# Two Gram matrices mirrored through DRAM instead of by TensorE, the second one moved ahead of a projection tile, and the batch loop written out

## The reference, cut to what matters

```python
z_l = einsum('bnd,ed->bne', x, W_lang)
z_g = einsum('bnd,ed->bne', x, W_grav)
v   = einsum('bnd,ed->bne', x, W_V)
zn  = z_l / maximum(norm(z_l), EPS)
A_l = maximum(zn @ zn^T, 0) * not_eye
sq  = sum(z_g * z_g)
d2  = maximum(sq + sq^T - 2 * z_g @ z_g^T, 0)
A_g = exp(-d2 / (2 * sigma * sigma)) * not_eye
K   = w_l * rownorm(A_l * adj) + (1 - w_l) * rownorm(A_g * adj)
out = layernorm(x + (K @ v) @ W_O^T)
```

## Time and profile before

| | |
|---|---|
| runs | 1014.73 us median of 3 (1011.64 to 1014.81) |
| the profiled execution: its own time, its span | 1013.06 us, 1011.3 us |
| mean granted TensorE clock | 0.996 |
| busy: PE, PEld, DVE, ACT, POOL | 983.0, 845.0, 677.1, 327.0, 151.7 us |

### The profile page before, as it was taken

One profiled execution on the slowest core, in us unless ns is written; L12 is line 12 of the kernel. 1 busy time (PEld: TensorE's weight loads), 2 busy tenths in 40 slices (PEclk: granted clock), 3 DMA queues, 4 the chain that ended last, 5 costly groups with the idle time before them and its releaser, 6 DMA issues.

```text
span 1011.3 us, 14938 instructions
## 1 busy us (share of the span) xinstructions
PE 983.0 (97%) x4970; PEld 845.0 (84%) x4970; DVE 677.1 (67%) x1842; ACT 327.0 (32%) x632; POOL 151.7 (15%) x155
## 2 busy tenths in 40 slices
PE   9999999999999999999999999999999999999997
PEld 7788887888888888888888888878898788888985
DVE  4555848657595675847757587565956758487488
ACT  4233233232332323224232342323323232342331
POOL 1202111021200212102121010212002121020231
PEclk9999999999999999999999999999999999999999
DMA  8320512415034250522405124150342504223001
GB/s 214 77 43 11 135 64 84 125 38 136 34 96 113 70 138 0 124 85 83 125 12 148 49 83 125 48 131 30 90 117 78 131 0 118 89 83 126 1 21 63
DMA packets 195698, 84.41 MB, mean 83 GB/s; under 512 B 138304, under 2 KB 171072, under 8 KB 195648
## 3 DMA queue, kind: packets, MB, share of 16 engines
q1 hardware_dynamic: 193536, 82.87, 30.0%
q10 hardware_dynamic: 2112, 1.05, 0.4%
HBM read 52.43 MB, written 31.46 MB: 83 GB/s over the span
## 4 chain that ended last, share of the span: by engine, by line
issue 66%; PE 18%; POOL 11%; DVE 3%; POOLq 0%; ACT 0%; DVEq 0%
POOL mask_r L1073 6%; PE ring L319 4%; PE ring L321 4%; PE ring L320 4%; POOL rstd L1080 3%; PE g_bank L321 2%; PE g_bank L320 2%; PE g_bank L319 2%; POOL r L1067 1%; POOL u_odd_lo L1055 1%; PE g_bank L314 1%; PE g_bank L357 0%; DVE bn L901 0%; DVE al L863 0%; DVE y L894 0%
## 5 line engine op out<-in xcount | busy, mean ns | idle before, releaser
L610 ACT ACTIVATE off<-g_bank 128x128 f32<-128x128 f32 (+1 forms) x128 | 40.4, 331 | 228.6 <-DVE diag_out L776 228.2
L1080 POOL TENSOR_TENSOR rstd<-var_eps,neg_half 128x1 f32<-128x1 f32 x64 | 45.8, 716 | 400.7 <-DVE var_eps L909 400.7
L700 DVE TENSOR_TENSOR zl_lo<-ring,zl_hi 128x512 fp32r<-128x512 f32 x64 | 44.1, 690 | 90.0 <-ACT zl_hi L559 90.0
L319 PE MATMUL ring<-xT_hi,wgT_hi 128*128 128x512 f32 x256 | 102.3, 399 | 0.3 <-DVE wgT_lo L725 0.3
L319 PE MATMUL ring<-xT_hi,wlT_hi 128*128 128x512 f32 x256 | 101.4, 396 | 0.0
L320 PE MATMUL ring<-xT_lo,wgT_hi 128*128 128x512 f32 x256 | 100.3, 392 | 0.0
L321 PE MATMUL ring<-xT_hi,wgT_lo 128*128 128x512 f32 x256 | 100.3, 392 | 0.0
L321 PE MATMUL ring<-xT_hi,wlT_lo 128*128 128x512 f32 x256 | 99.9, 390 | 0.0
L320 PE MATMUL ring<-xT_lo,wlT_hi 128*128 128x512 f32 x256 | 99.8, 390 | 0.0
L319 PE MATMUL ring<-wvo_hi,xT_hi 128*128 128x512 f32 x256 | 99.7, 389 | 0.0
L321 PE MATMUL ring<-wvo_hi,xT_lo 128*128 128x512 f32 x256 | 99.6, 389 | 0.0
(11 more groups left out here) (124 smaller groups left out, 2228.6 us busy)
## 6 DMA issues: line engine op xcount, KB each, us to landing
xb<-in_x_dram SPq DMA_DIRECT2D x60, 256.0 KB, 4.3
out_dram<-y SPq DMA_DIRECT2D x60, 256.0 KB, 2.8
k_turned<-ag SPq DMA_DIRECT2D x56, 256.0 KB, 2.0
al<-k_turned SPq DMA_DIRECT2D x224, 64.0 KB, 2.1
y<-in_x_dram SPq DMA_DIRECT2D x14, 1024.0 KB, 5.5
y<-in_x_dram SPq DMA_DIRECT2D x4, 256.0 KB, 5.2
al<-in_L_gnn_W_grav_dram ACTq DMA_DIRECT2D x4, 256.0 KB, 6.0
ag<-in_L_gnn_W_lang_dram SPq DMA_DIRECT2D x1, 1024.0 KB, 9.8
```

The lines of the kernel that those rows point to most:

```text
L319: nc.tensor.matmul(psum, lh, rh, start=k == 0, stop=False)
L610: nc.scalar.activation(off[:, mine[0]:mine[-1] + 1, :], g_bank[i][:, j0 * P:(j0 + len(mine)) * P] .rearrange("p (c n) -> p c n", n=P), ACT ...
L700: nc.vector.tensor_tensor(pair[1][:, i, :], bank[:, :], pair[0][:, i, :].bitcast(F32), ALU.subtract).then_inc(evacuated, 1)
L1080: nc.gpsimd.tensor_tensor(rstd[:, i:i + 1], var_eps[:, i:i + 1], neg_half[:, 0:1], ALU.pow)\
```

## The change

The loop over fourteen batches is written out in full on every engine, so that counts are constants. In these batches (not in the last two) VectorE transposes the blocks beside the diagonal in 32 x 32 blocks into `off` right after each diagonal, SP stores `off` to DRAM (384 KB) and loads it back in four pieces with the 32 x 32 blocks in their transposed places, and ScalarE copies the result from `off` into the banks, bank by bank; the exponent of a row tile waits for its own bank. TensorE mirrors nothing in them. The second Gram matrix stands ahead of the last `zg` tile instead of behind it, and the norms' row `r` ahead of the first `zl` tile. The orders of ScalarE, VectorE and SP are written anew for these batches.

```diff
-BATCH = ([("zg", 1, 0), ("hsq", 0, 0), ("zg", 1, 1), ("zg", 1, 2), ("zg", 1, 3), ("zl", 1, 0), ("r", 0, 0),
+BATCH = ([("zg", 1, 0), ("hsq", 0, 0), ("zg", 1, 1), ("zg", 1, 2), ("zg", 1, 3), ("r", 0, 0), ("zl", 1, 0),
...
-            with engine.Fori(0, (B - 2) // 2) as pair:
-                for parity in range(2):
-                    b = pair * 2 + parity
-                    batch(b, parity, Stream(BATCH, b * per + n_pro, b * per_split + n_pro, parity * per % RING))
+            for b in range(B - 2):
+                batch(b, b % 2, Stream(BATCH, b * per + n_pro, b * per_split + n_pro, b * per % RING))
...
+            def turn_off(which, b, rows_done):
+                g = ("g", "l").index(which)
+                sp.wait_ge(rows_done, b * T + T)
+                sp.dma_start(off_turned[g], off_wide).then_inc(off_stored, 16)
+                sp.wait_ge(off_stored, b * 32 + (g + 1) * 16)
+                for d in range(QN):
+                    sp.dma_start(off_wide[d * Q:(d + 1) * Q, :].rearrange("j (b r) -> j b r", b=QN),
+                                 off_by_part[g, d]).then_inc(off_loaded, 16)
...
+            def batch(b, parity, stream):
+                turn_off("g", b, gg_off)
+                load_x(b + 2)
+                turn_off("l", b, gl_off)
+                if b:
                     load_residual(b)
                 turn_k(b)
                 store_rows(b)
...
                 s.gram_g(0)
                 s.project("zg", 0)
-                s.mirror_g(0)
-                for i in range(1, T):
-                    s.project("zg", i)
+                s.hsq_as_rows(0)
+                s.project("zg", 1)
+                s.project("zg", 2)
                 s.gram_l(0)
-                s.project("zl", 0)
-                s.mirror_l(0)
+                s.project("zg", 3)
                 s.r_as_rows(0)
-                for i in range(1, T):
+                for i in range(T):
                     s.project("zl", i)
...
+                def copy_mirrors(self, which, done, banks):
+                    act.wait_ge(off_loaded, self.b * (32 * QN) + (16 * QN) * (("g", "l").index(which) + 1))
+                    mirrored = off_wide.rearrange("p (b s i) -> p s b i", b=QN, i=Q)
+                    for j in banks:
+                        mine = [s for s, (_, c) in enumerate(OFF_BLOCKS) if c == j]
+                        i0 = OFF_BLOCKS[mine[0]][0]
+                        nc.scalar.activation(
+                            g_bank[j][:, i0 * P:(i0 + len(mine)) * P].rearrange("p (s b i) -> p s b i", b=QN, i=Q),
+                            mirrored[:, mine[0]:mine[-1] + 1, :, :], ACT.Copy).then_inc(done, 1)
...
+                        if turned is not None:
+                            mine = [s for s, (a, _) in enumerate(OFF_BLOCKS) if a == i]
+                            j0 = OFF_BLOCKS[mine[0]][1]
+                            nc.vector.transpose(
+                                off_wide.rearrange("p (d s i) -> p s d i", d=QN, i=Q)[:, mine[0]:mine[-1] + 1],
+                                g_bank[i][:, j0 * P:(j0 + len(mine)) * P]).then_inc(turned, 1)
...
+                    if copied:
+                        dve.wait_ge(gg_copied, self.rows(db, i))
...
+                s.turn_k(3)
+                s.lo("u", 1, 0, u_next)
+                s.lo("u", 1, 1, u_next)
+                s.lo_k(0)
+                s.lo("u", 1, 2, u_next)
+                s.lo_k(1)
+                x_transpose(b + 2, 0)
+                s.lo("u", 1, 3, u_next)
```

More of the change, by code:

```diff
@@ L211, in graph_attention @@
         k_loaded = [sem(f"k_loaded{i}") for i in range(T)]
+        off_turned = nc.dram_tensor("off_turned", [2, P, len(OFF_BLOCKS) * P], F32).ap()
+        off_by_part = off_turned.rearrange("g (b j) (d r) -> g d j b r", j=Q, d=QN)
+        off_wide = off[:, :, :].rearrange("p s n -> p (s n)")
         block = ctx.enter_context(nc.Block())
@@ L275, in load_x @@
                 load_blocks(xb, x_blocks[b], xb_loaded)
[L277 to L279 removed]
+            def batch(b, parity, stream):
[3 more added lines that the diff above has]
+                if b:
                     load_residual(b)
                 turn_k(b)
[L283 to L284 removed]
                 store_rows(b)
[L286 removed]
             def last_two(b, stream):
+                load_residual(b)
                 sp.wait_ge(whole_transposed, b * T + 2 * T)
@@ L293, in last_two @@
                 store_rows(b + 1, y_last)
[L295 to L301, removed]
+            all_batches(sp, batch, last_two)
             sp.wait_ge(stored, 16 * T * B)
@@ L770, in lo, with diagonals @@
                     split_lo(ring[self.stream.bank(name)], self.stream.split_upto(name), pair, i)
-                def diagonals(self, db, rows_done, factor, col, done, row_tiles=range(T)):
+                def diagonals(self, db, rows_done, factor, col, done, row_tiles=range(T), turned=None):
                     for i in row_tiles:
@@ L828, in scale_first_mask, with mask_al @@
                         .then_inc(first_mask_r_ready, 1)
-                def mask_al(self, db, i):
-                    if i == 0:
-                        dve.wait_ge(gl_full, (self.b + db) + 1)
+                def mask_al(self, db, i, copied=False):
+                    if copied:
+                        dve.wait_ge(gl_copied, self.rows(db, T - 1))
+                    elif db == 0 and self.b < B - 2:
+                        pass
+                    elif i == 0:
+                        dve.wait_ge(gl_full, db + 1)
                     if db == 0:
@@ L914, in normalise, with batch @@
                                             ALU.subtract, ALU.mult).then_inc(y_done, 1)
-            def until_zl(s):
+            def batch(b, parity, stream):
+                s = Steps(b, stream)
+                u_next = u[1 - parity]
+                s.diagonals(0, gg_rows, 0.5, hsq, gg_diag, turned=gg_off)
+                s.lo("zg", 1, 0, zg)
+                s.repeat_row("hsq", 0)
+                s.lo("zg", 1, 1, zg)
+                for i in range(T):
+                    s.exponent(0, i, copied=True)
+                s.mask_ag(0, 0)
+                s.lo("zg", 1, 2, zg)
+                s.diagonals(0, gl_rows, 1.0, nsq, gl_diag, [0], turned=gl_off)
+                s.mask_ag(0, 1)
+                s.mask_ag(0, 2)
+                s.diagonals(0, gl_rows, 1.0, nsq, gl_diag, [1], turned=gl_off)
+                s.mask_ag(0, 3)
+                s.diagonals(0, gl_rows, 1.0, nsq, gl_diag, [2], turned=gl_off)
+                s.scale_of_ag(0)
+                s.diagonals(0, gl_rows, 1.0, nsq, gl_diag, [3], turned=gl_off)
+                s.clamp_norms(0)
+                s.lo("zg", 1, 3, zg)
+                s.repeat_row("r", 0)
+                s.lo("zl", 1, 0, zl)
+                s.mask_al(0, 0, copied=True)
+                s.mask_al(0, 1)
+                s.lo("zl", 1, 1, zl)
+                s.mask_al(0, 2)
+                s.mask_al(0, 3)
+                s.scale_of_al(0)
+                s.combine(0, 0)
+                s.lo("zl", 1, 2, zl)
+                s.turn_k(0)
+                s.combine(0, 1)
+                s.combine(0, 2)
+                s.turn_k(1)
+                s.combine(0, 3)
+                s.turn_k(2)
+                s.lo("zl", 1, 3, zl)
+                s.turn_k(3)
[6 more added lines that the diff above has]
+                s.lo("u", 1, 3, u_next)
+                for i in range(T):
+                    if i + 1 < T:
+                        x_transpose(b + 2, i + 1)
+                    whole_lo_part(b + 2, i, xT)
+                    s.residual(0, i)
+                    s.row_sums(0, i)
+                    if i + 2 < T:
+                        s.lo_k(i + 2)
+                    s.statistics(0, i)
+                    if i:
+                        s.normalise(0, i - 1)
+                s.normalise(0, T - 1)
@@ L941, in until_zl @@
                 s.scale_of_al(0)
[L943 to L979, removed]
                 s.lo("u", 1, 0, u[1])
```

70 lines of the change are left out of this document (48 added, 22 removed).

## The result

The changed kernel takes 998.93 us, the median of four runs (996.95 to 999.21), beside 1014.11 us for the kernel before on the same chip: a ratio of 0.985, 95% interval 0.9829 to 0.9872. The prediction was 1000 us. The profiled execution of the changed kernel has a span of 997.0 us and a time of 998.76 us of its own.

What follows compares the result with a forecast made beforehand. The prediction took TensorE to set the pace, busy 59.76 of 60.04 us in an ordinary batch. From 1013.06 us, - 18.5 - 15.1 + 16.0 + 4 gave 999.5, stated as 1000 us, range 989 to 1012.

Steps and rivals of the forecast that it cites:

- Term 1, the mirrors: Two runs of six TensorE mirrors, 0.66 us each run, leave each of fourteen batches: -18.5 us.
- Term 2, the loop: Straight code has no jumps, so the stalls behind them go: -15.1 us, or 0 if straight code stalls as much.
- Term 3, VectorE's order: At batch end VectorE stands behind ScalarE's high part of K tile 1; each batch ends 1.14 us later: +16.0 us.
- Term 4, the round trip: First Gram's trip through DRAM brings the first exponent about 0.3 us late per batch: +4 us, bounds 0 and 21.
- the low bound: Round-trip loads with uncontended landing, 2.1 us each and issued in 1.80, take 3.5 us instead of 4.0; cost 0.
- The prediction's own sign: The second Gram's first product waiting over 1.2 us for the exponent would mean the forecast is wrong.
- The order costs nothing: Rival: VectorE's new order at the batch end adds no time; 983.5 us, chance 0.08.
- The slow round trip: Rival: DMA landings under load come over 1.2 us a batch late, so the kernel is no faster; chance 0.13.
- Straight code stalls too: Rival: the written-out loop gains only about half of its term; 1007 us, chance 0.08.
- The clock: Rival: more waits of about a microsecond let TensorE fall to 1.2 GHz in every batch; 1016 us, chance 0.04.

Runs made afterwards that it cites:

- Experiment 1: The changed kernel with VectorE's order at the end of a batch put back as in the kernel before; 981.66 us, 0.9683 of the kernel before.
- experiment 3: The kernel before with its loops, SP's too, written out and nothing else changed; 998.61 us, 0.9858 of the kernel before.
- experiment 4: The kernel before, loop and mirrors kept, with only VectorE's order at the end of a batch taken from the changed kernel; 1034.82 us, 1.021.
- experiment 2: The changed kernel with ScalarE making the high part of K tile 1 ahead of that of u tile 3; 978.33 us, 0.9653 of the kernel before.
- experiment 6: The changed kernel with 16 idle TensorE transposes ahead of the prologue's `wvo` tiles, shifting its later code; a single run, 994.04 us.
- experiment 8: experiment 7 plus 16 idle TensorE transposes ahead of the prologue's `wvo` tiles; 970.79 us, 0.958 of the kernel before.
- experiment 7: experiment 2 with VectorE's low parts of K tiles 2 and 3 ahead of residual and row sums of output tiles 0 and 1; 973.86 us, 0.9607.
- experiment 5: Experiment 1 with the second Gram back behind the last `zg` tile and the norms' row behind the first `zl` tile; 981.71 us, 0.9689.

## Why the prediction was right

**Term 1, the mirrors, -18.5 us: right.** Experiment 1's ordinary batch is 58.70, that of the kernel before 60.03: 1.33 each, against 2 x 0.66 = 1.32, and both wait 0.4 for `kT_lo`.

**Term 2, the loop, -15.1 us: right.** Alone it measured -14.3 (experiment 3), and no wait of VectorE is put down to "issue" in the changed kernel. The bound that straight code stalls as much is excluded. The Trainium skill (Runtime: NRT & Kernel Launch, Instruction fetch mechanics) says that a taken branch out of the window forces a fetch before execution can go on, and that code streamed in order is fetched in 16 KiB blocks, mostly hidden. The changed kernel's trace agrees: 38 blocks came, and the stalls of 3.40 and 2.35 us that stood behind a jump have no successor. A block fetched in passing can still delay another transfer, as the DMA view of batch 4 shows.

**Term 3, VectorE's order, +16.0 us: right, in mechanism and in size.** Standing 1.43 us behind ScalarE's high part (1.4 said), delays of TensorE that grow by 1.16 (1.14 said), batches longer by 1.10: 14 x 1.10 = 15.4. Experiment 1 takes it out, experiment 4 puts it into the kernel before, experiment 2 shows that ScalarE's order is its cause. The text gave the two waits as 0.9 and 0.7; measured as gaps they are 0.89 and 0.39. That is a matter of reading: I worked out delays and compared them with gaps, which are 0.16 smaller, and I had the first delay too small (about 0.8, measured 1.05) and so the second too large (0.7, measured 0.55).

**Term 4, the round trip, +4 us: the size about right, the reasoning wrong.** The sum wanted the exponent 0.3 us late in every batch; in eleven batches it comes 0.6 early. Store and landing were as worked out: with 0.11 taken for the earlier start of batch 1, the last transpose was done at 126.5 (said 126.5) and the store had landed by 128.9 (129.1). The loads went by the low bound (3.5, from issue to ScalarE's first copy), not by K's loads (4.0), and the first exponent was done near 133.5, not 134.2. The cost arose elsewhere: in three batches a fetch of TensorE's code meets the round trip. The three are 1.65, 0.51 and 1.46 us above an ordinary batch, 3.6 together. So this step's mechanism failed, and that the sum still came out is luck: +4 spread evenly became 0 with three outliers. Batch 4 (store late by 2 us) and batch 7 (last load late by 0.9) are shown in the DMA views; batch 11 has a store landing in 4.3 us with a fetch beside it, and experiments 6 and 8 shift which batches are long. The prediction's own sign, that a wait of over 1.2 us for the exponent makes the forecast wrong, was met in batch 4 alone (a gap of 1.41); over the fourteen batches these gaps average 0.2.

**The sum by spans.** 1011.3 - 18.5 - 15.1 + 15.4 + 3.6 = 996.7, measured 997.0; the first two terms are the predicted ones. The fourteen batches alone went from 855.54 to 840.95 us, 14.6 less, which is the same sum. The last two batches, in which VectorE's order was changed a little as well (two low parts of `zl` tiles moved ahead of masked similarities), take 97.3 us in place of 97.1.

**The rivals.** *The order costs nothing* would have been 983.5; experiment 1, with that order undone, measures 981.66. *The slow round trip* (over 1.2 us a batch) did not happen; its mechanism, DMA landings delayed by others, is the right one for three batches. *Straight code stalls too* fell with experiment 3. *The clock* stayed at 1.00 in all fourteen batches of the changed kernel, so its short waits alone did not bring the slow level; but experiment 4 suggests that the pair of waits is not harmless where a wait of 2 us follows. One sum in the prediction's range does not come out: 995 to 1017 follows from the bounds of term 4 alone; with term 2 at its bound of 0, too, the top would be 1032.

## What to carry to other kernels

When one engine's queue is given a new order, lay the order of the engine that feeds it beside it: 1.1 us a batch, nearly the whole gain of the mirrors, went to an instruction moved ahead of what its producer still had queued, and swapping two lines of ScalarE gave it all back. A transfer with a margin of half a microsecond, repeated often enough, meets the background traffic of the program itself; look at the outliers among equal batches before the mean, and at the DMA view for single packets at the end of a transfer. Judge a change of several parts by its parts: here writing the loop out was worth as much as the whole.

## What the runs showed of the hardware

A fetch of 16 KB of TensorE's code that meets a store of 384 KB can make it land in 3.9 to 4.9 us where 2.3 is usual (changed kernel, experiments 1, 7 and 8): in batch 4 of the changed kernel and batch 7 of experiment 8 the bulk moves at its usual rate, and up to eight packets of 3 KB, one DMA engine's share, come singly afterwards. How late depends on where the two meet (experiments 5 and 6 have no store over 3.0); I did not work out a rule. The Trainium skill (DMA: Bandwidth & Descriptors, Queues, rings and completion order) says that an engine takes turns among its queues a packet at a time; one packet of 16 KB that took 1.62 us, with packets of 3 KB behind it, fits that, though no run here varied the sizes and nothing here shows that the packets of the Trainium skill are those of the view.

The kernel before, given two short waits a batch (0.89 and 0.41 us) in place of one (0.28 in batch 1), met the 1.2 GHz level behind five of six waits of 2 us in place of one of six, some 2 us each time. In experiment 7 a single wait of 1.84 us was followed by a slow stretch, in the changed kernel one of 1.41 was not. What decides between them stays open.
